# A four-layer graph network on one core: the stretch between the edge ranking and the first walk, with fp16 masks in four buffers, and with loads, turns and gathers in another order

## What is computed

```python
h = maximum(layernorm(x), 0); x = x + layer_d(h, src, dst)      # d = 0..3
# layer 0: twice  segment_sum((h * norm_src @ W)[src], dst) * norm_dst + b   (3,125-row form of a graph conv, here on 50,000)
# layer 1: concat(h, mean of h[src] per dst) @ W.T + b
# layer 2: two SAGE convolutions, 128 -> 256 -> 128
# layer 3: gelu(concat(h[src], h[dst], edge_weight) @ We1 + be1) @ We2 summed by dst, then an update net and a layernorm
```

## Time and profile before

| | before |
|---|---|
| median of three runs | 5160.67 us |
| the profiled execution's own time | 5161.02 us |
| its span, first to last instruction | 5159.0 us |
| TensorE busy | 4072.5 us (79%) |
| VectorE busy | 3400.9 us (66%) |
| ScalarE busy | 2990.4 us (58%) |
| GpSimd busy | 3073.0 us (60%) |
| mean granted TensorE clock | 0.912 |

### The profile page before, as it was taken

The page is one execution under the profiler, slowest core; times in us unless marked ns, Lnnn a source line. Parts: engine busy times, 40 slices in busy tenths (PEclk is TensorE's granted clock), DMA queues, the critical chain, the costliest instruction groups (busy, mean ns, idle before and its releaser), DMA issues. The chain is left out here.

```text
span 5159.0 us, 130637 instructions
## 1 busy us (share of the span) xinstructions
PE 4072.5 (79%) x23084; PEld 3055.8 (59%) x23085; DVE 3400.9 (66%) x12207; ACT 2990.4 (58%) x6766; POOL 3073.0 (60%) x3244
## 2 busy tenths in 40 slices
PE   6967775777689996766699999978888177777777
PEld 2334443777677775656577777767776155555555
DVE  9989995555478885777333333347777257777777
ACT  6835552666567775666454545546666155556555
POOL 0057772777577765777544444347664677777771
PEclk9989997999889997887799999999999589999998
DMA  1023331666556665887555555558877366666664
GB/s 23 0 62 102 104 103 60 197 212 198 175 167 199 199 198 173 261 256 245 167 178 177 174 180 176 172 180 270 268 266 257 102 180 199 202 201 197 198 198 143
DMA packets 599695, 905.37 MB, mean 175 GB/s; under 512 B 98488, under 2 KB 254280, under 8 KB 599600
## 3 DMA queue, kind: packets, MB, share of 16 engines
q1 hardware_dynamic: 467072, 670.37, 39.2%
q0 software_dynamic: 100352, 180.83, 14.3%
q10 hardware_dynamic: 32176, 53.17, 2.8%
HBM read 491.31 MB, written 412.69 MB: 175 GB/s over the span
## 5 line engine op out<-in xcount | busy, mean ns | idle before, releaser
L1020 PE MATMUL banks<-M,OH 128*128 x7840 | 1200.8, 311 | 383.4 <-POOLq L599 206.6
L570 POOL DMA_INDIRECT M<-table_a,six x1176 | 1125.4, 957 | 428.0 <-issue 324.5
L1020 PEld LDWEIGHTS banks<-M,OH 128*128 128x128 f32 x7840 | 1085.2, 213 | 431.4 <-issue 417.5
L570 POOL DMA_INDIRECT M<-table_b,six x784 | 767.1, 978 | 541.7 <-PE banks L1017 305.8
L659 ACT ACTIVATE AG<-banks x1176 | 632.3, 589 | 598.7 <-PE banks L1020 553.8
L565 POOL DMA_INDIRECT edges_by_block<-pack,pos_i x392 | 377.7, 964 | 417.2 <-DVE pos_i L1292 303.5
L677 ACT ACTIVATE HO<-H,BI,SC 128x128 f32 (+1 forms) x1176 | 484.0, 482 | 105.7 <-DVE BI L1453 58.6
L1406 DVE TENSOR_TENSOR OH<-banks,dstrel 128x1024 f32<-128x1024 f32 x392 | 478.8, 1222 | 85.5 <-PE banks L1020 72.2
L659 ACT ACTIVATE T<-banks 128x512 f32<-128x512 f32 (+1 forms) x588 | 294.7, 518 | 340.9 <-DMA table_a<-T 312.6
L570 POOL DMA_INDIRECT M<-table_pairs,dix x392 | 400.8, 1023 | 119.5 <-issue 100.0
L570 POOL DMA_INDIRECT M<-table_pairs,six x392 | 378.5, 966 | 128.2 <-issue 111.9
(11 more groups left out here) (313 smaller groups left out, 8321.2 us busy)
## 6 DMA issues: line engine op xcount, KB each, us to landing
XZ<-state SPq DMA_DIRECT2D x490, 256.0 KB
table_a<-T SPq DMA_DIRECT2D x294, 256.0 KB
state<-T SPq DMA_DIRECT2D x294, 256.0 KB
state<-H SPq DMA_DIRECT2D x196, 256.0 KB
h_turned<-HT ACTq DMA_DIRECT2D x196, 256.0 KB
table_pairs<-T SPq DMA_DIRECT2D x98, 512.0 KB
M<-messages SPq DMA_DIRECT2D x98, 512.0 KB
XZ<-in_x SPq DMA_DIRECT2D x194, 256.0 KB
```

Source lines behind the costliest of these rows:

```text
L570: nc.gpsimd.indirect_dma_start(out=M[:, slot, :], out_offset=None, in_=table, in_offset=bass.IndirectOffsetOnAxis(ap=idx, axis=0)).then_in ...
L1020: last = mm(banks[:, ds(sums_at[k], P)], OH[:, b * US + k, :], source[:, ds(rows_at[k], P)], start=False, stop=False, skip_group_check=True)
```

## The change

- The mask buffer `ge` becomes fp16 with four places, the matrix of ones is the fp16 one, and the three kinds sum into three PSUM banks (0, 1, 2). So VectorE makes the first four masks without a wait, and from then on waits for the product four masks back. `b_row` and `ls_row` are read when all twelve masks are made. TensorE no longer waits for `s_t1` ahead of the mask products, but ahead of the products of the step places. The semaphore `s_tabr` goes.
- The four loads of `e_in`, with the two waits for all scatters, move from SyncE to GpSimd, right behind its scatters.
- The twelve turns become a function `sorted_fields(k)`. The four of the sources run ahead of the walk tables, the other eight where all twelve were. They use banks 4 and 5.
- GpSimd waits ahead of phase 0 for `s_er >= 4` (sources read) in place of `s_rel` and `s_tq`. These two waits stand at chunk 8 of phase 0, where the ring of 32 tiles is full.
- `M` is the first buffer in the space given back, ahead of `AG`.

```diff
@@ -217,7 +217,7 @@
         dgT = tmp("dgT", [BC, W4]); rgT = tmp("rgT", [BC, W4])
-        ge = tmp("ge", [BC, 512])
+        ge = tmp("ge", [BC, 4, 512], F16)
         b_row = tmp("b_row", [P, STEPS]); t_bc = tmp("t_bc", [BC, STEPS]); t_cl = tmp("t_cl", [1, STEPS])
...
@@ -238,8 +238,9 @@
 
+        M = sb("M", [P, RING, P])
         AG = sb("AG", [P, (AGR + 1) * W4])
-        M = sb("M", [P, RING, P]); OH = sb("OH", [P, 2 * US, P])
+        OH = sb("OH", [P, 2 * US, P])
         H = sb("H", [P, 2, 2, W4])
...
@@ -257,7 +258,7 @@
         s_dg = sem("degree_rank_order"); s_dgt = sem("degree_rows"); s_dgc = sem("degree_rows_read"); s_dr = sem("degree_rows_stored")
-        s_tabm = sem("table_products"); s_tabr = sem("table_reads"); s_ge = sem("table_masks")
+        s_tabm = sem("table_products"); s_ge = sem("table_masks")
         s_diag = sem("diag_made"); s_base = sem("rank_bases"); s_rk = sem("rank_onehots")
...
@@ -397,10 +398,6 @@
             staggered(sp, [(1, load0), (9, store0)])
-            for k in range(2):
-                sp.wait_ge(s_scat[k], 16 * TILES // 2)
-            for k in range(Q4):
-                sp.dma_start(e_in[:, k, :], edges.rearrange("(k t p) f -> k t (p f)", k=Q4, p=P)[k]).then_inc(s_el, 16)
             sp.wait_ge(s_rel, 1)
...
@@ -566,6 +563,11 @@
 
+            for k in range(2):
+                pool.wait_ge(s_scat[k], 16 * TILES // 2)
+            for k in range(Q4):
+                nc.gpsimd.dma_start(e_in[:, k, :], edges.rearrange("(k t p) f -> k t (p f)", k=Q4, p=P)[k]).then_inc(s_el, 16)
+
             def gather(table, idx, slot, done):
...
@@ -624,6 +626,11 @@
                     elif not isinstance(turn, int) or 16 * turn + c >= per:
+                        if ph == 0 and not isinstance(turn, int) or c != 8:
+                            pass
+                        elif ph == 0:
+                            pool.wait_ge(s_rel, 1)
+                            pool.wait_ge(s_tq, 17)
                         if c % 8 == 0 or not vals:
...
@@ -648,8 +655,7 @@
 
-            pool.wait_ge(s_rel, 1)
-            pool.wait_ge(s_tq, 17)
+            pool.wait_ge(s_er, Q4)
             for ph in range(6):
...
@@ -952,23 +958,18 @@
             staggered(pe, [(0, ranked), (8, products(0, w1[:, :])), (6, turn_rows(0, HO))])
-            pe.wait_ge(s_t1, GROUPS)
-            n = 0
-            for kind in range(3):
-                w = TABW[kind]
-                if kind >= 2:
-                    pe.wait_ge(s_tabr, kind - 1)
-                for c in range(Q4):
-                    pe.wait_ge(s_ge, n + 1)
-                    n += 1
-                    mm(ps[6 + kind % 2][:, 0:w], ones[0:BC, :], ge[:, 0:w], start=(c == 0), stop=(c == Q4 - 1)).then_inc(s_tabm, 1)
-
-
+            for n in range(3 * Q4):
+                kind, c = divmod(n, Q4)
+                pe.wait_ge(s_ge, n + 1)
+                mm(ps[kind][:, 0:TABW[kind]], ones_h[0:BC, :], ge[:, c, 0:TABW[kind]], start=(c == 0), stop=(c == Q4 - 1)).then_inc(s_tabm, 1)
+
+            pe.wait_ge(s_rr, GROUPS * CH + 2)
             for n in range(3 * Q4):
                 pe.wait_ge(s_ec, n + 1)
                 if n >= 2:
                     pe.wait_ge(s_er, n - 1)
-                nc.tensor.transpose(ps[n % 2][:, 0:BC], e_f[:, :], ident[0:BC, 0:BC]).then_inc(s_et, 1)
+                nc.tensor.transpose(ps[4 + n % 2][:, 0:BC], e_f[:, :], ident[0:BC, 0:BC]).then_inc(s_et, 1)
+            pe.wait_ge(s_t1, GROUPS)
             for c in range(Q4):
...
@@ -1294,23 +1295,38 @@
 
-            n = 0
-            for kind in range(3):
+            for n in range(3 * Q4):
+                kind, c = divmod(n, Q4)
                 lo = 512 * kind if kind < 2 else 0
+                if kind:
+                    dve.wait_ge(s_tabm, n - 3)
+                col = (first if kind == 2 else start)[:, c:c + 1]
+                v.tensor_scalar(ge[:, c, 0:TABW[kind]], iota_f[0:BC, lo:lo + TABW[kind]], col, None, ALU.is_ge).then_inc(s_ge, 1)
+            for kind in range(2):
+                lo = 512 * kind
+                dve.wait_ge(s_tabm, (kind + 1) * Q4)
+                v.tensor_scalar(b_row[:, lo:lo + TABW[kind]], ps[kind][:, 0:TABW[kind]], -1.0, None, ALU.add)
+            dve.wait_ge(s_tabm, 3 * Q4)
+            link(v.scalar_tensor_tensor(ls_row[:, :], ps[2][0:1, 0:TILES], -1.0, iota_f[0:1, 0:TILES], ALU.add, ALU.add))
+
+            def sorted_fields(k):
                 for c in range(Q4):
+                    n = k * Q4 + c
+                    part = slice(c * BC, (c + 1) * BC)
                     if n:
-                        dve.wait_ge(s_tabm, n)
-                    n += 1
-                    col = (first if kind == 2 else start)[:, c:c + 1]
-                    v.tensor_scalar(ge[:, 0:TABW[kind]], iota_f[0:BC, lo:lo + TABW[kind]], col, None, ALU.is_ge).then_inc(s_ge, 1)
-                dve.wait_ge(s_tabm, n)
-                got = ps[6 + kind % 2]
-                if kind < 2:
-                    ins = v.tensor_scalar(b_row[:, lo:lo + TABW[kind]], got[:, 0:TABW[kind]], -1.0, None, ALU.add)
-                else:
-                    ins = v.scalar_tensor_tensor(ls_row[:, :], got[0:1, 0:TILES], -1.0, iota_f[0:1, 0:TILES], ALU.add, ALU.add)
-                link(ins)
-                dve.sem_inc(s_tabr, 1)
+                        dve.wait_ge(s_et, n)
+                    field = e_in[:, c, :].rearrange("t (p f) -> t p f", f=4)[:, :, k]
+                    v.tensor_copy(e_f[:, :], field.bitcast(F32) if k == 2 else field).then_inc(s_ec, 1)
+                    if k == 1:
+                        v.tensor_copy(e_dst[:, c, :], field)
+                    dve.wait_ge(s_et, n + 1)
+                    got = ps[4 + n % 2][:, 0:BC]
+                    if k == 0:
+                        v.tensor_scalar(src2T[:, part], got, 2.0, None, ALU.mult)
+                    v.tensor_copy((srcT, dstT, ewT)[k][:, part], got).then_inc(s_er, 1)
+
+            dve.wait_ge(s_el, 64)
+            sorted_fields(0)
             by_win = lambda t: t.rearrange("o (w k) -> o w k", k=US)
...
@@ -1354,21 +1370,8 @@
 
-            dve.wait_ge(s_el, 64)
-            for n in range(3 * Q4):
-                k, c = divmod(n, Q4)
-                part = slice(c * BC, (c + 1) * BC)
-                if n:
-                    dve.wait_ge(s_et, n)
-                field = e_in[:, c, :].rearrange("t (p f) -> t p f", f=4)[:, :, k]
-                v.tensor_copy(e_f[:, :], field.bitcast(F32) if k == 2 else field).then_inc(s_ec, 1)
-                if k == 1:
-                    v.tensor_copy(e_dst[:, c, :], field)
-                dve.wait_ge(s_et, n + 1)
-                got = ps[n % 2][:, 0:BC]
-                if k == 0:
-                    v.tensor_scalar(src2T[:, part], got, 2.0, None, ALU.mult)
-                v.tensor_copy((srcT, dstT, ewT)[k][:, part], got).then_inc(s_er, 1)
+            sorted_fields(1)
+            sorted_fields(2)
             for c in range(Q4):
```

## The result

The changed kernel takes **5099.84 us**, the median of four runs from 5096.3 to 5103.13, against 5161.07 for the kernel before in four runs beside it (5158.96 to 5166.88). The ratio is 0.9883, with a 95% interval of 0.987 to 0.9895: 61 us less. Forecast were 5109.5, in a range from 5101 to 5124. The profiled run took 5097.1 us with a span of 5095.3.

The account below looks back on a forecast made before the run. No engine bounds the whole kernel: a serial chain after ranking, then GpSimd's gathers in phase 0. Chain 19.8 plus early gathers 33.9 less contention 2.2 gave -51.5 from 5161.02: 5109.5 us, range 5101 to 5124.

Parts of the forecast that it names:

- Masks: Mask rounds after ranking: four masks hide behind TensorE's drain, the rest is VectorE's own work; `ls_row` over 19.9 us earlier.
- Loads: `e_in` loads issued by GpSimd after its scatters: landed by 811 us, wanted at 816.9, so costed at nothing.
- Rival C: `e_in` loads from GpSimd's queue take 4 us each and land about 5 us late: 5115 us; chance 0.03.
- Sources, first gather: Source fields ahead of the walk tables: done at 821.4 us, index copy follows, first gather starts at 822.6.
- Rival D: First gather waits for something else, such as all of `table_a`; only the chain's 19.8 us are gained; chance 0.02.
- The chain behind: Tables, destinations, weights and step places follow the sources; 33rd gather 53.7 us earlier, before 2.2 us for contention.
- VectorE and GpSimd together: 69 VectorE instructions from the sources to `s_rel` run beside the first gathers: 2.2 us lost.
- Rival B: VectorE instructions wait out gathers: half of one each, 5140 us, chance 0.05; a whole one each, 5172, chance 0.02.
- Does the lead last?: Phase 0: windows catch up after 30 to 45 of 98, then follow the gathers; GpSimd stays 53.7 us ahead.
- waits for windows again and again: Sign of being wrong: GpSimd repeatedly waiting for windows in phase 0; only the first such wait was expected.
- The sum: Whole kernel: -53.7 us at the 33rd gather plus 2.2 for contention gives -51.5, so 5109.5 us.
- moves everything behind it as a block: From phase 1 to the end: everything after phase 0 shifts earlier by the same 51 us.

Follow-up runs that it names:

- run without lead: The changed kernel with GpSimd again waiting for the walk tables and stored steps ahead of phase 0: 5129.11 us against 5151.66 for the kernel before.
- loads by SyncE: The changed kernel with the four loads of `e_in` back on SyncE, behind its last store of `table_a`: 5105.82 us against 5157.38 for the kernel before.
- numbers in the gaps: The changed kernel with VectorE's six destination-number instructions moved into the waits between the step places: 5098.49 us, ratio 0.9883 to the kernel before.

## Why the prediction was right in its mechanism and missed in its size

**Masks.** Forecast -19.9. `ls_row` ends 14.3 us after the first mask, 35.6 before: -21.3 in the trace, -19 by the ratios of the two runs of this part alone. TensorE came out of the drain 0.5 us earlier, counted from the first mask, and the writing of fp16 costs what fp32 cost: a mask of 392 columns lasts 416 ns, 424 before. Four in a row overlap a little and take 1.42 us, 1.68 forecast.

**Loads.** Costed at nothing, and so it was. A load of GpSimd's occupies the engine for 2.29 / 4 = 0.57 us, less than the 1.3 that I had as a bound. The engine waited 4.34 us for the scatters to land, more than my two. The loads were out at 805.5, took 2.8 to 4.8 us from issue to landing, and had all landed at 809.7; they were wanted at 812.6. The cover was thus 2.9 us and not 6. Rival C falls.

**Sources, first gather.** Forecast 822.6, measured 819.74 with ranking over 2.75 us earlier: 21.6 and 21.5 us after the first mask. I missed that the index copy takes 1.63 us where it took 0.21; the shorter masks made up for it. Rival D, a first gather that waits for something else, falls as well.

**The chain behind.** Step places over 56.4 + 2.2 us after the first mask, measured 55.9. The 33rd gather: -53.7 + 2.2 = -51.5 forecast, -53.3 measured from the first mask (67.4 against 120.7).

**VectorE and GpSimd together.** Forecast 2.2 us. From `b_i` to the first `sel` the changed kernel takes 21.4 us where the run without lead takes 20.8, and the step places 15.7 where it takes 14.8: **1.5 us** in all for the 69 instructions and 32 gathers. The price per instruction at which the change would lose was 0.78 us; measured are 1.5 / 69 = 0.02. Rival B falls with both its prices. The index copy is the exception. It starts while VectorE works on `b_i`, and ends 0.07 us after the third VectorE instruction from there:

```profile
817.08 0.55 DVE L1332 CAST b_i<-b_row 1x784 int32<-1x784 f32 x1
817.56 0.34 DVE L1333 CAST ls_i<-ls_row 1x392 int32<-1x392 f32 x1
817.83 0.95 DVE L1334 TENSOR_TENSOR t_bc<-iota_f,b_row 98x784 f32<-98x784 f32 x1
```

In all twelve traces in which this copy runs under the tables it takes 1.63 us and ends 73 to 76 ns after `t_bc`. The Trainium skill (SBUF — State Buffer, "Who interferes with whom") states a lock by which the later of the two fully blocks for the whole instruction. The trace agrees for the copy; for the gathers it shows a rare stretching only, in the change's lead at most from 0.94 to 1.30 us.

**Does the lead last?** Yes. Between the 33rd and the last gather lie 470.2 us, 468.2 before. GpSimd waits for windows in phase 0 twelve times, 7.3 us together and at most 1.0, where I had said that only the first would do so:

```profile
POOL M L572 <- PE banks L1021: 7.3, 12, 1.0
```

(Waits of GpSimd in the changed kernel, 870 to 1336 us.) That fits the 2 us by which the lead shrank. One of my signs of being wrong, waits for windows again and again, did come, but it cost no more than this.

**The sum** for the stretch, -51.5, is what the trace has, with two small misses in it that cancel: the 33rd gather came 1.8 us better than forecast, and phase 0 gave 1.8 back. That it agrees to 0.1 us is luck: the wait for `table_b` that closes the stretch alone differs from 24.6 to 28.1 us between the five traces. **The step that failed is the last one: that a gain of phase 0 "moves everything behind it as a block", with a range whose low end lay only 8.5 us below the forecast and held terms of the stretch alone.** The work before and behind the stretch is not constant. Between traces with the same code there, ranking ends between 797.7 and 801.8 us, and phase 4 takes 599 to 610. In the changed kernel's profiled run both fell on the good side (-2.75 and -8.1 against the trace of before), and that is the -12 beyond the stretch, but for 1 us (phases 1 to 3 gave 2.5 and the end took 1.1). I had read one trace of before, and took what lies outside the edit as fixed, although it is 4540 of 5160 us. (A slip beside it: rival D, at some 5141, lies outside the range too, so the chance of a time outside was 0.15 by my own list and not 0.13.)

Is it only spread? Not within the first measurement: its interval means 54 to 67 us, and 51.5 lies outside. Over the four kernels of the first kind, the measured difference less that of the stretch is -9.7 us for the change (-61.2 and -51.5), -3.4 with the loads by SyncE (-51.6, -48.2), -2.2 with the numbers in the gaps (-58.9, -56.7) and +1.8 without lead (-22.5, -24.3). The sign isn't constant and the mean is -3.4. The spread is as wide as what is asked for: the four executions with the loads by SyncE lie 16 us apart, those with the numbers in the gaps 22. All twelve timed executions of the change and its two close relatives average some 58 us below the befores beside them. The stretches of these three account for 52 of them. So a good part of the 10 us is probably difference between executions and occasions; it was not measured again on the first kind with the change itself. A lasting remainder of 3 to 6 us, in phases 1 to 3 for instance, isn't excluded and stays open.

## What to carry to other kernels

A queue that paces a phase should start as soon as its first operands exist: its buffers' depth in lead (here 32 gathers) is work done under a serial chain, and here it was kept to the end of the phase within 2 us, the consumers being faster than the queue. Size the move from event to event, from the trace, and keep a second term for the rest of the kernel: a sum that is right to the us in the edited stretch still misses by what untouched stages vary between executions, which one profile of before can't show. Shortening a chain by a buffer per round also moves the due times of the loads behind it, so they have to be moved with it.

## What the runs showed of the hardware that I had not expected

- The same kernel takes 5160 us on some occasions and 6510 on others, where VectorE and ScalarE wait some 6 us at a time in their loops, for nothing that a row names (212 us in 34 waits of one VectorE line, within 600 us), while straight code without gathers beside it is as fast.
- On those chips two waits of 4 to 10 us stand in the straight code of the step places in all five traces in which gathers run beside it, and in none of the ten others; the step places were over 16 us later.
- A GpSimd copy of 128x32 int32 took 1.63 us, until 0.07 us after the third of three VectorE instructions in a row, in twelve traces of twelve, and mostly 0.21 elsewhere. 69 VectorE instructions beside 32 gathers lost 1.5 us in all.
- A load of 98x512 int32 issued by GpSimd occupies it for 0.57 us and lands 2.8 to 4.8 us after issue, a gather of 128 rows for 0.94 and 1.25 from start to start.
- Phase 4 of the walk, 600 us of the same instructions, varied by 10 us with TensorE's mean granted clock between 0.93 and 0.95.
